# Three steps of two engines and one row of pacing digits, moved in a four-layer convolution and attention kernel

## The reference, cut to what matters

```python
x = x + L0(gn(x))          # mLSTM block, linear, 3x3 convolution, batch norm, leaky relu
x = x + L1(gn(x))          # 6 heads of attention over 1024 positions, 32 channels each
x = x + L2(gn(x))          # deformable 3x3 depthwise convolution: 4 corners gathered per tap
x = x + L3(gn(x))          # gated feed-forward: 2x2 FFT filter, 3x3 depthwise, gelu gate
```

## Time and profile before

| what | us |
|---|---|
| median of 3 executions | 8503.88 |
| lowest and highest | 8468.47, 8513.41 |
| the profiled execution | 8503.88 |
| its span, first to last instruction | 8502.1 |

### The profile page before, as it was taken

The page is one execution under the profiler, slowest core; times in us unless marked ns, Lnnn a source line. Parts: engine busy times, 40 slices in busy tenths (PEclk is TensorE's granted clock), DMA queues, the critical chain, the costliest instruction groups (busy, mean ns, idle before and its releaser), DMA issues.

```text
span 8502.1 us, 101634 instructions
## 1 busy us (share of the span) xinstructions
PE 7694.5 (91%) x37966; PEld 3896.7 (46%) x37966; DVE 5840.1 (69%) x9918; ACT 3724.1 (44%) x7236; POOL 2207.8 (26%) x1798
## 2 busy tenths in 40 slices
PE   7999999999999987699999999999999999999977
PEld 4555555555555542244344344344344344344343
DVE  4676666666766664576686686687687687686664
ACT  4555555555555534334334434334434434434410
POOL 1222222222222210033134134134134134134152
PEclk9999999999999987799999999999999999999989
DMA  1111111111111120154354454354454454454365
GB/s 65 39 38 38 43 43 49 47 43 41 38 38 43 44 98 4 52 145 157 107 153 156 112 148 155 107 149 160 116 140 158 114 141 158 116 140 158 108 199 140
DMA packets 244236, 850.14 MB, mean 100 GB/s; under 512 B 46412, under 2 KB 49176, under 8 KB 243360
## 3 DMA queue, kind: packets, MB, share of 16 engines
q1 hardware_dynamic: 150272, 388.71, 17.0%
q0 software_dynamic: 92160, 453.06, 16.9%
q10 hardware_dynamic: 1312, 1.87, 0.1%
HBM read 602.10 MB, written 89.68 MB: 81 GB/s over the span
## 4 chain that ended last, share of the span: by engine, by line
PE 38%; DVE 16%; DMA 4%; issue 4%; ACT 3%; POOL 1%; SPq 1%; DVEq 0%; ACTq 0%; POOLq 0%
PE ps L2282 6%; PE ps L2734 5%; DVE arena L1962 5%; PE ps L2515 4%; PE ps L389 4%; DMA arena<-img,arena 3%; PE ps L2713 3%; PE ps L2745 2%; PE ps L2202 2%; PE ps L2269 2%; PE ps L2186 2%; PE ps L2399 2%; POOL arena L2548 1%; DVE arena L2443 1%; PE ps L2229 1%
## 5 line engine op out<-in xcount | busy, mean ns | idle before, releaser
L2548 POOL DMA_INDIRECT arena<-img,arena x1152 | 1410.8, 1225 | 2618.8 <-DMA img<-arena 1749.2
L1962 DVE TENSOR_REDUCE arena<-ps 128x2 f32<-128x1024 f32 x768 | 894.5, 1216 | 331.5 <-PE ps L2245 328.7
L2124 ACT ACTIVATE arena<-ps 128x512 f32<-128x512 f32 x1536 | 822.3, 598 | 361.5 <-PE ps L2269 287.1
L2443 DVE SCALAR_TENSOR_TENSOR arena<-arena 128x384 f32<-128x384 f32 x1152 | 744.3, 647 | 277.2 <-DMA arena<-img,arena 261.4
L998 POOL TENSOR_TENSOR arena<-arena 128x512 f32<-128x512 f32 x384 | 443.2, 1161 | 1757.0 <-DMA arena<-decay 1756.8
L2282 PE MATMUL ps<-arena 128*64 128x512 f32 x3072 | 850.4, 634 | 32.5 <-DVE arena L1980 17.1
L2734 PE MATMUL ps<-arena 128*64 128x512 f32 x3072 | 791.4, 638 | 72.8 <-ACT arena L2692 38.2
L2515 PE MATMUL ps<-arena 128*96 128x128 f32 x4608 | 608.2, 288 | 98.7 <-DVE arena L2432 91.5
L2515 PEld LDWEIGHTS ps<-arena 128*96 128x96 f32 x4608 | 550.8, 172 | 305.2 <-issue 259.1
L389 PE MATMUL ps<-arena 128*128 128x256 f32 x2432 | 598.6, 398 | 11.4 <-DVE arena L2883 10.1
L389 PEld LDWEIGHTS ps<-arena 128*128 128x128 f32 x2432 | 470.1, 198 | 159.0 <-issue 81.8
(11 more groups left out here) (350 smaller groups left out, 12634.6 us busy)
## 6 DMA issues: line engine op xcount, KB each, us to landing
arena<-arena SPq DMA_DIRECT2D x1024, 144.5 KB
arena<-decay SPq DMA_DIRECT2D x384, 256.0 KB, 3.2
img<-arena SPq DMA_DIRECT2D x162, 384.0 KB, 2.6
arena<-img,arena POOLq DMA_INDIRECT x1152
arena<-y SPq DMA_DIRECT2D x16, 768.0 KB, 6.4
arena<-x SPq DMA_DIRECT2D x16, 768.0 KB
out<-arena SPq DMA_DIRECT2D x16, 768.0 KB
arena<-x SPq DMA_DIRECT2D x16, 512.0 KB, 5.0
```

The lines of the kernel that those rows point to most:

```text
L1962: dve.tensor_reduce(out, self.wides[B.at("max", b, g, n, h) // 2].rearrange("p (a b) -> p a b", a=2), AX.X, AL.max).then_inc(*S.mark("max_ ...
L2124: act.activation(self.p[n % 6], B("score", b, n)[:, :], ACT.Exp).then_inc(*S.mark("p_act", b, n))
L2443: dve.scalar_tensor_tensor(gb[:, 0:384], gb[:, 384:768], pp[:, 1, n:n + 1], gb[:, 0:384], AL.mult, AL.add).then_inc(*S.mark("corner_x", b, n))
L2548: pool.indirect_dma_start(self.g[n % 6], None, img, bass.IndirectOffsetOnAxis(ap=ii[:, n:n + 1], axis=0)).then_inc(*S.landed(f"{self.tag}g ...
```

## The change

Three constants and one row of digits. `dve_add` for the next image moves from t = 41 to t = 44 on VectorE (there after the eviction of that step), `act_affine` moves from t = 37 to t = 40 on ScalarE (there after the exponentials of that step, and now behind `finish(0)` instead of ahead of it). Both hold for all images. In the second row of `PACE` sixteen digits change, all between t = 24 and t = 53.

```diff
@@ class Layer1: def dve
             if t == 39:
                 finish(0)
-            if t == 41:
+            if t == 44:
                 self.dve_add(dve, b + 1)
@@ class Layer1: def act
             if t == 38:
                 finish(0)
-            if t == 37:
+            if t == 40:
                 self.act_affine(act, b + 1)
@@ PACE, second row, second half (digit 64 to 127)
-        "1331111003000000033300000000082000002032200101404100000020202030",
+        "1331111003000000033300000000082000200411100101710100000403000002",
```

## The result

The changed kernel takes 8550.14 us (median of 6, 8544.67 to 8567.21), the kernel before 8497.38 us (median of 6, 8468.47 to 8515.79). The ratio, which rests on 24 executions of the changed kernel, is 1.0069, with a 95% interval of 1.0054 to 1.0085: 0.7% slower. That is 58 us by the ratio and 53 between the medians, where 25 were forecast.

What follows compares the result with a forecast made beforehand. No single bound: TensorE and VectorE hand the path to each other. 14.6 + 5.5 + 5.2 + 0 + 0 = 25.3 us on 8503.9 gave 8529 us, 0.3% slower; forecast's own range 8512 to 8545, stated range 8480 to 8560.

Steps and rivals of the forecast that it cites:

- slower beyond measurement: Rival: TensorE's clock falls in all eleven blocks, ScalarE's affine makes TensorE late to group 3; 8558 us, chance 17%.
- Part 1: Digits t = 24 to 30: TensorE's step 27 slips behind group 0's sums, 1.33 us in eleven blocks, 14.6 us.
- Part 2: TensorE's clock during group 0's sums: three more blocks pay 1.8 us each for the lower level, 5.5 us.
- upper bound of 12.6: Most the clock term could cost, in us: all seven blocks that do not pay today would pay.
- Part 3: Digits t = 36 to 38 on VectorE: eviction of t = 36 behind n = 25, 0.4 us a block, 5.2 us.
- part 5: Digits from t = 45 on, VectorE: evictions of t = 50 and 52 between n = 34 and 35; taken as 0.
- Part 4: VectorE's `dve_add` behind the evictions of t = 42 and 44: same sum of durations, nothing added.
- Part 6: ScalarE and TensorE from t = 36: affine loses its cover, step 44 ends 1.2 us later, hidden; costed at nothing.
- cover of 4.02 us: TensorE's stand ahead of group 3, waiting for VectorE's weighing; taken as room that absorbs TensorE's delays from t = 36 on.
- From t = 34 on VectorE is the path: From the eviction of t = 34 to group 3's weighing VectorE bounds; TensorE has 4.02 us to give away.

Runs made afterwards that it cites:

- Experiment 3: Changed kernel with the add ahead of the eviction within t = 44, so the copy stands between add and interpolations: 1.0025 of the kernel before.
- experiment 4: Kernel before with only the digits of t = 24 to 30 changed (2004111 for 0020322): 1.0041, 8501 against 8473 us.
- experiment 7: Kernel before with the digits of t = 24 to 30 changed and six dummy matmuls on TensorE ahead of the wait for group 0's weighing: 1.0021.
- experiment 5: Kernel before with only the digits of t = 36 to 38 changed (7 1 0 for 4 0 4): 1.0011.
- Experiment 2: Kernel before with only the moves, act_affine at t = 40 and dve_add at t = 44, old digits: 1.0039, +33 us.
- Experiment 11: Kernel before with dve_add at t = 33 and act_affine at t = 27, old digits: 1.0011.
- the digits together: Kernel before with all sixteen digits changed and neither move: 1.0016, 8484 us against 8473.
- experiment 10: Kernel before with three dummy matmuls on TensorE ahead of the wait for group 0's weighing, behind step 27: 1.0046.

## Why the prediction was right or wrong

The time lies in the stated range, and the direction is right. But the forecast of the likeliest, 25 us, is less than half of what was measured, and the loss of more than 0.5% had been given a chance of 0.22 only. The 8550 also lie above the forecast's own range (8512 to 8545). That they lie in the stated one is luck: it reached so far for the rival "slower beyond measurement", whose reason was not what happened. Experiment 3, the change without the held gather, shows how good the other terms were: 21 us (8 to 34) where the sum had 25.

*Part 1, the slipped step: right.* TensorE's order, the wait of 2.5 us and the place of step 27 are as described, and experiment 4 shows the piece to be the costly one among the digits. Its count was a little high: it took eleven blocks to have a stand between step 27 and the sums, but in the kernel before the first sum record has none in blocks 7, 8 and 11.

*Part 2, the clock: right in kind, too few records counted.* Three more blocks were to pay 1.8 us each. In fact the 24 records run slowly in all thirteen blocks (3.85 to 5.41 us, 4.69 in the mean), where the kernel before has four slow sums of 18 records. At the full clock 24 records take 2.84 us, so the records alone lose 24 us against 7 before. The error was to carry over both the 1.8 us of 18 records and the number of blocks. Not all of it reaches the time. Parts 1 and 2 together had 20.1 us, and the span from step 24 to step 34 grew by 22 (experiment 4), so the two terms were about right together. The 17 us of experiment 7 are the whole price of the low clock in the new order, of which the kernel before pays some 7 already; they do not show that the upper bound of 12.6 was passed. How the 22 us divide between the slipped step and the clock, and what ScalarE's late exponentials around t = 30 add, the runs do not tell.

*Part 3 and part 5, the evictions among the interpolations: not contradicted.* Alone they measure 0.11 and 0.07%, with intervals that hold the forecast 5 us and nothing. The 0.4 us that part 3 expected between the eviction of t = 34 and the weighing of group 2 can't be made out: this stretch takes 15.1 us before, 15.3 after and 15.1 in experiment 5.

*Part 4, the moved add: the step that failed.* "The sum is the same if the evictions need not be waited for. ... So nothing is added." The sum of VectorE's own durations is indeed the same; the changed timeline has the forecast order without a gap. What was missing is another engine. The two evictions had stood between the add and the interpolations, and they had a part that no duration shows: behind them GpSimd's gather is done in 1.08 us. Straight behind the add it takes 3.99, and VectorE's n = 33 waits 3.7 us for it instead of 0.8. Part of that is saved at the next gathers, so that 2.4 us a block or 31 us are lost against the kernel before. Experiment 2 costs 33 us by the moves alone. Experiment 3 gives 37 back by one swap, which fits the 3.0 us a block by which it is ahead of the changed kernel in this stretch. The rows for it were there: GpSimd's gathers take 0.95 us in some places and over 2 in others in the kernel before, and I had looked at when they were released, not at how long they take.

*Part 6, ScalarE and the cover of 4.02 us: right for the forecast.* TensorE stands 1.15 us at t = 42 for the exponentials, where some 2 were expected. Ahead of group 3 it stands even longer than before, since the gathers are late; compare:

```profile
7206.14 4.59 PE L389 MATMUL ps<-arena 128*128 128x256 f32 x20
7216.80 5.43 PE L2515 MATMUL ps<-arena 128*96 128x128 f32 x24 [6.07 <-DVE arena L2432]
```

*"From t = 34 on VectorE is the path": only for delays.* The held gather shows that a delay of VectorE there is paid for. Experiment 11 shows that the reverse fails: taking the add's 4.9 us out of VectorE's way there gains nothing, since TensorE's last `back` is a second path of nearly the same length. The 4.02 us of the earlier trace rows are room behind the last `back`, not ahead of it; part 6 was only saved by the fact that VectorE came later still.

*Of the rivals,* "slower beyond measurement" gave the nearest time (8558) for a reason of which half was there: the clock in every block, but not ScalarE's lateness reaching group 3. The extra 31 to 37 us came from a mechanism that stood in no rival.

What stays open: why the digits together (0.16%) cost less than their first piece alone (0.41%), what brings ScalarE's late exponentials, most of the loss of experiment 10, and what exactly ends the hold of a gather.

## What to carry to other kernels

When an operation is moved along an in-order engine, its own duration and its waits are not all: look at what now stands next to what, and at the duration of the other engines' instructions there, above all GpSimd's gathers. A row whose mean hides two values (1.1 and 4.0 us here) is worth a look at its single instances before an order is called free. And a stand of one engine is room only for work behind its last hand-over: where two engines alternate as the path, shortening one of them may only move the wait.

## What the runs showed of the hardware

A gather issued by GpSimd (an indirect DMA) was held through a whole unbroken run of VectorE on on-chip memory: 3.98 to 3.99 us instead of 1.07 to 1.08, in 13 of 13 blocks, ending 0.82 us after VectorE stops. Whether this gather was held depended on what VectorE had done just before the run. After two evictions out of the accumulators, or a copy of 32x1 out of them, it took 1.08 us, though the same interpolations were under way; after the two-input add, or after the add and a 96x1 copy within on-chip memory, it was held.

That is no rule for every gather. In the kernel before, the next one (n = 34) was held until 0.82 us after VectorE stopped in six blocks, and in seven got through while VectorE went on, with the same instructions around it. And a gather can be held by one instruction alone. In block 12 of the changed kernel, n = 32 ends at 7192.35, which is 0.82 us after the end of the weighing (7191.53), while VectorE goes on with finish:

```profile
7190.35 2.00 POOL L2548 DMA_INDIRECT arena<-img,arena  x1 [0.30 <-issue]
```
```profile
7189.57 1.96 DVE L2432 TENSOR_TENSOR arena<-arena 128x1728 f32<-128x1728 f32 x1
7191.44 1.21 DVE L1986 TENSOR_TENSOR arena<-arena 96x1024 f32<-96x1024 f32 x1
```

The Trainium skill has a frame for this on its page "SBUF — State Buffer", section "SBUF: two separate sides": VectorE and GpSimd share a pair of ports as an exclusive lock, held for the whole instruction, and a DMA issued by GpSimd waits because its descriptors can't be written while VectorE has the pair. The trace agrees in that held gathers end just behind an instruction of VectorE. The page names VectorE's two-port modes for this; of an instruction with two inputs from on-chip memory it says only that it contends with a GpSimd instruction that reads there. Here such two-input instructions (the weighing, the interpolations) held gathers. A lock of one instruction would also not explain a hold through eight of them, of 0.4 to 0.6 us each. In both points the measurement decides. That the port is the cause at all is argued from the page and not shown, since the port is in no trace.

In block 12 of the changed kernel TensorE's clock was at the full level (2.4 GHz) ahead of this place and fell to the lower one (1.2 GHz) when TensorE stood for 2.3 us ahead of `back` and, after 1.4 us of it, for 2.5 us ahead of the sums. The 24 sum records then took 4.5 us, where 24 such records at the full clock take 2.8. Six dummy matmuls in the second wait brought 17 us back. Three of them in the old order, at a place that TensorE reaches when the wait is over, went with a loss of 0.46%, of which they explain only a part.
